# Streamed-block loads issued by GpSimd instead of the sync engine

## The reference

```
x = x + L0(_gn(x))      # causal-masked depthwise convolution, 6 x 11 taps per channel
x = x + L1(_gn(x))      # qk + bias: bias[c, i, j] = table[i - j], table from a small MLP
```

## Time and profile before

| | |
|---|---|
| median of three runs | 3039.08 us |
| the profiled execution | 3043.68 us, span 3041.9 us |
| busy, share of the span | PE 68%, DVE 76%, ACT 55%, POOL 39% |
| moved by DMA | 916.61 MB, mean 301 GB/s |
| the two large queues | q1 (SP) 595.03 MB, q10 (ACT) 318.80 MB |
| streamed loads | 192 from the input and 96 from the output, 512.0 KB each |
| streamed stores | 288, in the middle 6.2 us from issue to landing |

### The profile page before, as it was taken

How to read it: one execution, slowest core, us unless ns; L and a number is a source line. 1 busy time by engine, 2 the same in 40 slices (tenths; PEclk the granted TensorE clock), 3 DMA queues, 4 the chain that set the end, 5 groups by cost and what they waited for, 6 DMA issues and landing times.

```text
span 3041.9 us, 81453 instructions
## 1 busy us (share of the span) xinstructions
PE 2063.3 (68%) x28880; PEld 1942.9 (64%) x28880; DVE 2305.0 (76%) x4167; ACT 1675.7 (55%) x3051; POOL 1178.2 (39%) x1988
## 2 busy tenths in 40 slices
PE   3199877777677766777767776777767777878600
PEld 0098867666666666666656776766666667778600
DVE  6789887788778777787776887868877777757634
ACT  2067655655465554655556565565555656676611
POOL 0023243534335243443444344343433435554433
PEclk9999989888799888988889988899989998998855
DMA  8876769999798997999889997999989997788799
GB/s 259 293 274 199 256 211 336 332 325 316 275 341 311 324 329 267 333 325 315 285 303 341 326 318 265 352 335 316 313 287 332 330 324 261 257 280 276 263 331 338
DMA packets 471917, 916.61 MB, mean 301 GB/s; under 512 B 39280, under 2 KB 39280, under 8 KB 469584
## 3 DMA queue, kind: packets, MB, share of 16 engines
q1 hardware_dynamic: 308448, 595.03, 58.1%
q10 hardware_dynamic: 163200, 318.80, 28.3%
HBM read 594.18 MB, written 319.68 MB: 300 GB/s over the span
## 4 chain that ended last, share of the span: by engine, by line
DMA 41%; DVE 22%; issue 17%; PE 7%; ACT 6%; POOL 3%; SPq 2%; ACTq 1%; DVEq 0%; POOLq 0%
DMA ubuf<-in_x 13%; DMA out<-kept_c_band 11%; DVE entries L699 6%; DMA out<-ubuf 6%; PE psY L1011 5%; DMA abuf<-in_x 5%; DVE kept_c_band L837 4%; DVE XT L671 4%; DMA kept_c_band<-in_x 3%; DVE psY L684 3%; ACT junk L555 2%; POOL ubuf L946 2%; DVE kept_c_band L686 2%; DMA ubuf<-out 2%; PE psT L997 2%
## 5 line engine op out<-in xcount | busy, mean ns | idle before, releaser
L1011 PEld LDWEIGHTS psY<-wsplit,XT 128*128 128x128 f16 x25920 | 1649.6, 103 | 365.9 <-DVE XT L671 98.3
L1011 PE MATMUL psY<-wsplit,XT 128*128 128x168 f16 (+5 forms) x25920 | 1678.7, 226 | 288.1 <-DVE kept_c_band L686 156.4
L671 DVE TENSOR_TENSOR XT<-psT,XT 128x512 f16<-128x512 f32 x720 | 490.9, 682 | 436.1 <-ACT XT L533 435.3
L997 PE MATMUL psT<-ident,xn 128*128 128x128 f32 x2880 | 508.3, 304 | 398.7 <-POOL xn L915 268.4
L946 POOL TENSOR_TENSOR ubuf<-ubuf,bias 128x1024 f32<-128x1024 f32 x184 | 423.1, 2300 | 704.4 <-ACT ubuf L577 704.4
L533 ACT CAST XT<-psT 128x512 f16<-128x512 f32 x720 | 414.1, 575 | 502.4 <-PE psT L997 339.5
L699 DVE BATCH_NORM_STATS2 entries<-abuf 128x6 f32<-128x512 f32 x928 | 587.5, 680 | 89.6 <-DMA abuf<-in_x 88.1
L915 POOL TENSOR_TENSOR xn<-xn,mask 128x512 f32<-128x512 f32 x336 | 421.1, 1253 | 466.0 <-ACT xn L518 394.0
L997 PEld LDWEIGHTS psT<-ident,xn 128*128 128x128 f32 x2880 | 335.8, 153 | 413.4 <-POOL xn L915 272.2
L938 POOL COPY halo<-XT 128x16 f16<-128x16 f16 x720 | 232.0, 322 | 661.1 <-DVE XT L671 647.9
L577 ACT ACTIVATE ubuf<-ubuf,outp 128x1024 f32<-128x1024 f32 x184 | 210.2, 1143 | 476.2 <-DMA ubuf<-in_x 351.6
(11 more groups left out here) (76 smaller groups left out, 434.2 us busy)
## 6 DMA issues: line engine op xcount, KB each, us to landing
abuf<-in_x SPq DMA_DIRECT2D x464, 512.0 KB, 8.2
out<-ubuf ACTq DMA_DIRECT2D x288, 512.0 KB, 6.2
kept_c_band<-in_x SPq DMA_DIRECT2D x112, 1024.0 KB, 7.8
out<-kept_c_band ACTq DMA_DIRECT2D x112, 1024.0 KB, 8.3
ubuf<-in_x SPq DMA_DIRECT2D x192, 512.0 KB, 7.6
band<-in_x SPq DMA_DIRECT2D x48, 1024.0 KB, 12.6
out<-band ACTq DMA_DIRECT2D x48, 1024.0 KB, 7.6
ubuf<-out SPq DMA_DIRECT2D x96, 512.0 KB, 8.0
```

The source lines that it names most:

```text
L671: nc.vector.tensor_tensor(XT[:, n % NB3, 1, :, 2:P + 2], psT[n % NB3][:, :, :], XT[:, n % NB3, 0, :, 2:P + 2], ALU.subtract).then_inc(lo_r ...
L997: last = nc.tensor.transpose(psT[m][:, i, :], xn[:, m, i, :, :].rearrange("p k c -> p (k c)"), ident[:, :])
L1011: last = nc.tensor.matmul(psY[m][:, 0:rows, o + lo_c:o + hi_c], XT[:, m, xp, i, 2 - sh:2 - sh + P], wsplit[:, c, wp, K * sh:K * sh + rows, ...
```

## The change

The loads of streamed half-blocks leave SP's list. The same waits and the same transfer stand in POOL's list as `load_stream`, at the same planned positions, behind POOL's masks, halo copies and `add_bias` of that position. Waits, buffers, sizes and positions stay as they are.

```diff
                     if do_c:
-                        for u in range(NU):
-                            if p.u_load[u] == n:
-                                (c, b, q), h = STREAM[u // 2], u % 2
-                                wait_alone(sp, u_stored[u % NUB], 16 * (gc * (NU // NUB) + u // NUB))
-                                spilled = q <= b
-                                if spilled:
-                                    wait_alone(sp, x1_spilled[(b, q)], 16 * (chan(gc, c) + 1))
-                                src = (ov if spilled else xv)[chan(gc, c), b]
-                                sp.dma_start(ubuf[:, u % NUB, :, :], src[:, 2 * h:2 * h + 2, BW * q:BW * (q + 1)]
-                                             ).then_inc(u_loaded[u % NUB], 16)
                         if n == BIAS_LOAD[1]:
...
+            def load_stream(g, u):
+                (c, b, q), h = STREAM[u // 2], u % 2
+                wait_alone(pool, u_stored[u % NUB], 16 * (g * (NU // NUB) + u // NUB))
+                spilled = q <= b
+                if spilled:
+                    wait_alone(pool, x1_spilled[(b, q)], 16 * (chan(g, c) + 1))
+                src = (ov if spilled else xv)[chan(g, c), b]
+                nc.gpsimd.dma_start(ubuf[:, u % NUB, :, :], src[:, 2 * h:2 * h + 2, BW * q:BW * (q + 1)]
+                                    ).then_inc(u_loaded[u % NUB], 16)
...
                         for u in range(NU):
                             if p.u[u] == n and not on_dve[u]:
                                 add_bias(gc, u)
+                        for u in range(NU):
+                            if p.u_load[u] == n:
+                                load_stream(gc, u)
```

## The result

The changed kernel takes 3234.02 us (median of four, 3225.40 to 3237.72) against 3039.68 us for the kernel before on the same chip: 1.0625 times as long, interval 1.0589 to 1.0661. The forecast was 3183 us with a range of 2980 to 3320; the sign and the range held, and 51 us of the loss were not foreseen. The profiled execution took 3233.92 us.

A forecast was written before the change was run, and what follows sets the result against it. No engine was full; waits between in-order engines set the time, with DMA close behind. Laps +59, stage before the last +21 and last stage +64 gave +144 us: 3188 profiled, 3183 as median; range 2980 to 3320.

The forecast's parts named there:

- last stage: After the last matmul, only finishing left: loads chained behind additions, 17 steps of 10.05 us, +64 us.
- first window's end: In each lap, half-block 17's load stands behind the addition of 16 and lands later: +4.8 us; 16 no later.
- second window: In each lap, half-blocks 24 to 35: four steps, two issues, landing and finish, 51.1 us against 43.4, +7.7 us.
- gains at 5 and 20: In each lap, these loads escape SP's kept-store and reload waits: 8.1 + 6.5 us earlier, half counted, -7.3 us.
- masks: In each lap, 15 loads directly ahead of a mask TensorE needs, a quarter of them waited for: +4.7 us.
- six laps: The six steady laps, each +9.9 us from windows, gains and masks: +59 us.
- stage before the last: Half-blocks 6 to 16 in 6 steps, +18.6 us; second window +7.7; less 5 for a stall: +21 us.
- four steps from 24 to 32: In a lap's second window, the steps to half-blocks 26, 28, 30 and 32: 41.8 us.
- c: GpSimd's price for issuing a load, including any later start of the transfer: taken as 1.25 us.
- L: A streamed load's landing time after its issue: taken as 5.5 us in the laps, 5.1 in the last stage.
- Faster: Rival: cheap issue (0.4 us) and landing of 4.3 us (3.9 last) on the separate queue; -52 us, 2987; chance 0.22.
- The queue is no help: Rival: landing stays 7.7 us (6.7 last) because the same DMA engines are shared; +292 us, 3331; chance 0.15.

The follow-up runs named there:

- experiment 1: Changed kernel, all streamed loads still on GpSimd but at the head of their position, ahead of masks, halo copies and additions: 3082.23 us, ratio 1.0130.
- experiment 2: Kernel before, SP issuing each streamed load only after the GpSimd addition it stood behind in the changed kernel: 3187.62 us, ratio 1.0471.
- experiment 3: Changed kernel, but SP issues the streamed loads of the last stage: 3161.89 us, ratio 1.0385.
- experiment 8: Kernel before, with GpSimd issuing only half-blocks 5, 20, 21, 22 of the six laps, behind the additions of their position: 3002.20 us, ratio 0.9884.
- experiment 9: Kernel before, with GpSimd issuing only half-blocks 20, 21, 22 of the six laps, behind the additions of their position: 3006.50 us, ratio 0.9899.
- experiment 10: Kernel before, with GpSimd issuing only half-block 5 of the six laps, behind the addition of its position: 3040.68 us, ratio 1.0013.
- experiment 4: Changed kernel, with GpSimd also clearing an unused spare tile behind each streamed load: 3223.74 us, ratio 1.0602.
- experiment 5: Changed kernel, with GpSimd clearing an unused spare tile ahead of each streamed load, which waits for it: 3355.07 us, ratio 1.1046.

## Why the prediction was right, and where it was off

The mechanism was the one predicted: a load at the same position of a busier in-order list is issued later, behind the additions there, and each half-block waits for the one before. Experiments 1 and 2 show it from both sides, and experiment 3 shows that the last stage's part is its own. By its terms (windows of a lap are means of four laps, from the end of one half-block's finish to the end of the other's):

| term | predicted | measured |
|---|---|---|
| last stage | +64 | +67.4 |
| first window's end, 8 to 17, a lap | +4.8 | +4.6 |
| second window, 24 to 35, a lap | +7.7 | +11.3 |
| gains at 5 and 20, a lap | -7.3 | +3.1 (4 to 8), -0.8 (17 to 24) |
| masks, a lap | +4.7 | 0 |
| six laps | +59 | +109.5 |
| stage before the last | +21 | +13.7 |
| sum | +144 | +190 |

*The step that failed* is the gain at 5 and 20: put at -7.3 us a lap, it came out as a loss of 2.3, and by it the laps. GpSimd did come earlier: 5 is finished 15.6 us after 4 where it was 22.0, 20 is finished 59.0 us after 18 where it was 63.6. But at 5 the half-blocks behind follow the same rule as the windows, which I had not applied to them: 6 stands behind the addition of 5, 7 behind that of 6. ScalarE's scaling of 5 and 6 in a lap after the change:

```profile
1632.99 1.15 ACT L567 ACTIVATE ubuf<-ubuf,outp 128x1024 f32<-128x1024 f32 x1 [0.96 <-DMA ubuf<-in_x]
...
1644.42 1.15 ACT L567 ACTIVATE ubuf<-ubuf,outp 128x1024 f32<-128x1024 f32 x1 [5.16 <-DMA ubuf<-in_x]
```

The addition of 5 and the load of 6 on GpSimd, one behind the other:

```profile
1634.47 1.99 POOL L946 TENSOR_TENSOR ubuf<-ubuf,bias 128x1024 f32<-128x1024 f32 x1
1636.41 0.75 POOL L937 DMA_DIRECT2D ubuf<-in_x  x1
```

VectorE's finish of 7 in the same lap:

```profile
1658.90 1.28 DVE L836 SCALAR_TENSOR_TENSOR ubuf<-ubuf,outp,bias 128x1024 f32<-128x1024 f32 x1 [4.30 <-DMA ubuf<-in_x]
```

Half-block 6 follows 5 by 11.43 us where it was 4.98, and from 5 to 7 there are 9.3 us more in the mean: the 6.4 us gained at 5 and 2.9 more.

Where these links are missing, little of the gain at 5 is kept either. In experiment 1 the loads of 7 and 8 land 5.5 and 5.7 us ahead of their use (means of four laps), so nothing there waits for a load, and yet from 4 to 8 the lap is only 1.7 us shorter than before the change. In a lap of that run VectorE stands for an input load and then works without a pause until it finishes 7:

```profile
1582.27 1.29 DVE L689 BATCH_NORM_STATS2 entries<-abuf 128x6 f32<-128x512 f32 x2 [4.18 <-DMA abuf<-in_x]
...
1592.53 1.28 DVE L836 SCALAR_TENSOR_TENSOR ubuf<-ubuf,outp,bias 128x1024 f32<-128x1024 f32 x1
```

These are the two reasons that I gave for halving the gain, input loads and VectorE next; half was too much to keep.

At 20 4.5 us are won and 1.9 more up to 22, and from 22 to 24 5.6 us are lost again. No addition holds the load of 24 there; it stands behind a halo copy that waits for VectorE. A halo copy and the load of 24 in a lap after:

```profile
1856.98 0.20 POOL L928 COPY halo<-XT 128x16 f16<-128x16 f16 x1 [3.93 <-DVE XT L661]
...
1857.81 0.72 POOL L937 DMA_DIRECT2D ubuf<-in_x  x1 [0.49 <-issue]
```

That load starts 123.9 us after the finish of 17 (mean of four laps), 123.1 before the change, and 117.0 and 116.6 in experiments 8 and 9, where SP issues it. With the others left on SP the gain from 17 to 24 is there: 7.2 and 6.4 us a lap, about the 6.5 us worked out from the earlier trace rows, whole and not half. It is a sum, though: in experiment 9 5.7 us are won at 20 and 4.4 up to 22, and 3.7 lost up to 24. At 5 alone there is nothing (experiment 10).

*The first window's end* has the right sum by luck. Half-block 17 follows 16 by only 2.7 us more, since its load landed 4.4 us from the start of its issue and not 6.75; and 16, which I had as no later, is 1.9 us later (means of four laps).

*The second window* was short in its tail. I put the load of 34 straight behind the addition of 32; but it is planned one position later, and a mask that waits for ScalarE stands between. Addition of 32, mask, loads of 34 and 35 in a lap after:

```profile
1909.04 2.35 POOL L946 TENSOR_TENSOR ubuf<-ubuf,bias 128x1024 f32<-128x1024 f32 x1 [1.63 <-ACT ubuf L567]
...
1914.87 1.12 POOL L905 TENSOR_TENSOR xn<-xn,mask 128x512 f32<-128x512 f32 x1 [3.48 <-ACT xn L508]
...
1916.20 1.47 POOL L937 DMA_DIRECT2D ubuf<-in_x  x2
```

The load starts 4.81 us after the addition's end instead of at once. The four steps from 24 to 32 were right: 42.7 us by ScalarE's starts in this lap, 41.8 predicted.

*Masks* cost nothing: TensorE's waits for them are 269.7 us against 268.4, and experiment 4 adds 0.65 us a load to them without a loss.

*The last stage* came out by the right number of links (17), and by luck in their price, since c and L were off against each other. *The stage before the last* was dearer in the prediction than on the chip: from 6 to 16 it is 58.8 us instead of 62.7, the step being 9.8 and not 10.45, and its second window lost 3.1 us instead of 7.7.

Of the rivals, *Faster* needed c + L under about 5.2 us; with 6.0 and 7.2 it was far from it. *The queue is no help* had the right reason in part, since the late loads of experiment 2 land as fast on SP's queue, but the wrong landing: loads issued later landed sooner, whoever issued them (7.2 and 6.1 us in the laps, against 7.9). Experiment 2 agrees with the Trainium skill, DMA: Bandwidth & Descriptors, "Issuing engines are not separate DMA queues", by which transfers of all issuers interleave on the same engines: the third issuer's loads landed no sooner than SP's (6.0 us against 5.4 in the last stage, 7.2 against 6.1 in the laps).

## What to carry to other kernels

When an instruction moves to another engine "at the same position", ask what stands ahead of it in that engine's list and what that waits for, above all whether any of it waits for what the moved instruction brings; then count the links, for every block and not only in the dense windows. A gain found at one block holds only if the blocks behind it come earlier too: moving the three loads around 20 in six laps gains 1%, moving all 36 of every group loses 6%, and moving 5 alone gains nothing, since 6 came 1 us earlier and 7 not at all. Price the two sides of a moved instruction apart, since 0.65 us of work behind the load was free and 1.36 us of delay ahead of it cost 121 us.

## What was not expected

GpSimd took 0.73 us to issue a 512 KB load where SP took 0.37, whichever tensor it read from. A wait of GpSimd on its own clearing of a tile cost 0.73 us a time (experiment 5), more than the clearing of 0.63. And freeing SP of 567 us of waits brought no gain that these runs show: 444 us more of waiting for VectorE's statistics took their place, and the laps of experiment 1, which lose nothing to additions at their own position, are as long as before.
